# Deltas of all three scan steps on TensorE, key products written in order, and `bn_aggr` for the statistics of the tail

## The reference

```python
def step(S, kvq):
    k_t, v_t, q_t = kvq
    k_norm = k_t / (jnp.linalg.norm(k_t, axis=-1, keepdims=True) + 1e-06)
    retrieved = jnp.einsum('bnij,bnj->bni', S, k_norm)
    delta = v_t - retrieved
    S_new = jnp.tanh(S + jnp.einsum('bni,bnj->bnij', delta, k_norm))
    Sq = jnp.einsum('bnij,bnj->bni', S_new, q_t).reshape(B_, n)
    out = Sq * jax.nn.silu(Sq)
    return (S_new, out)
```

```python
def _layernorm(x, axis=-1, eps=1e-05):
    m = jnp.mean(x, axis=axis, keepdims=True)
    v = jnp.var(x, axis=axis, keepdims=True)
    return (x - m) / jnp.sqrt(v + eps)
```

## Time and profile before

| | before |
|---|---|
| median of 3 runs | 1132.73 us (1132.68 to 1133.84) |
| the profiled execution's own time | 1132.0 us |
| its span, first to last instruction | 1130.1 us |
| mean granted TensorE clock | 0.996 |
| busy share of the span: PE, DVE, ACT, POOL | 97%, 84%, 52%, 45% |

### The profile page before, as it was taken

The page is one execution under the profiler, slowest core; times in us unless marked ns, Lnnn a source line. Parts: engine busy times, 40 slices in busy tenths (PEclk is TensorE's granted clock), DMA queues, the critical chain, the costliest instruction groups (busy, mean ns, idle before and its releaser), DMA issues.

```text
span 1130.1 us, 16851 instructions
## 1 busy us (share of the span) xinstructions
PE 1097.6 (97%) x5925; PEld 855.1 (76%) x5925; DVE 944.7 (84%) x1415; ACT 592.3 (52%) x988; POOL 512.2 (45%) x426
## 2 busy tenths in 40 slices
PE   9999999999999999999999999999999999999786
PEld 4566666678787777878778877878787788778575
DVE  4788888973034998999899889989998998899898
ACT  2345555555435355645655574556456555754544
POOL 1466677676333244324433432443244334364653
PEclk9999999999999999999999999999999999999899
DMA  7346555623531440423132323404231323231001
GB/s 262 109 158 246 205 202 201 247 100 112 168 112 49 139 130 19 130 80 127 56 113 83 123 74 111 148 19 124 81 128 51 116 78 108 75 112 57 1 1 40
DMA packets 45131, 127.03 MB, mean 112 GB/s; under 512 B 4368, under 2 KB 21520, under 8 KB 43152
## 3 DMA queue, kind: packets, MB, share of 16 engines
q1 hardware_dynamic: 43920, 114.20, 30.3%
q10 hardware_dynamic: 1152, 12.07, 2.9%
HBM read 117.86 MB, written 19.92 MB: 122 GB/s over the span
## 4 chain that ended last, share of the span: by engine, by line
PE 73%; DVE 16%; POOL 4%; issue 3%; ACT 2%; DMA 0%; SPq 0%; POOLq 0%; DVEq 0%; ACTq 0%
PE lower L1243 43%; PE bank L1243 17%; PE lower L440 5%; PE lower L572 2%; POOL state L748 2%; POOL rgn L757 2%; PE bank L1232 1%; DVE tmp L2290 1%; DVE tmp L2276 1%; PE bank L487 1%; DVE Sq L2278 1%; DVE tmp L2301 1%; DVE y L847 1%; DVE delta L2297 1%; DVE S L2303 1%
## 5 line engine op out<-in xcount | busy, mean ns | idle before, releaser
L2059 POOL TENSOR_TENSOR a_lo<-whole,a_hi 128x512 fp32r<-128x512 f32 x128 | 181.6, 1435 | 260.3 <-ACT a_hi L1644 172.4
L1243 PE MATMUL lower<-b_hi,ring 128*128 128x512 f32 x512 | 193.8, 396 | 1.4 <-ACT a_hi L1644 1.4
L1243 PE MATMUL lower<-b_lo,ring 128*128 128x512 f32 x512 | 190.9, 391 | 1.7 <-POOL b_lo L2059 1.7
L1243 PE MATMUL lower<-a_hi,ring 128*128 128x512 f32 x496 | 187.5, 394 | 0.0
L1243 PE MATMUL lower<-a_lo,ring 128*128 128x512 f32 x496 | 185.4, 390 | 0.0
L2059 POOL TENSOR_TENSOR b_lo<-whole,b_hi 128x512 fp32r<-128x512 f32 x64 | 93.5, 1469 | 144.4 <-ACT b_hi L1644 125.8
L1627 ACT ACTIVATE S<-S 128x1024 f32<-128x1024 f32 x56 | 58.6, 1059 | 172.8 <-DVE S L2303 168.9
L1643 ACT ACTIVATE whole<-lower,hs 128x512 f32<-128x512 f32 x126 | 86.2, 685 | 81.0 <-PE lower L1243 79.2
L1243 PEld LDWEIGHTS lower<-b_hi,ring 128*128 128x128 f32 x512 | 96.2, 188 | 21.9 <-issue 1.8
L1243 PEld LDWEIGHTS lower<-b_lo,ring 128*128 128x128 f32 x512 | 96.1, 188 | 21.9 <-POOL b_lo L2059 2.3
L440 PE MATMUL lower<-wa,xT 128*128 128x512 f32 x240 | 109.3, 599 | 2.1 <-DVE turned L817 1.4
(11 more groups left out here) (293 smaller groups left out, 2418.8 us busy)
## 6 DMA issues: line engine op xcount, KB each, us to landing
ring<-ffn_copy_dram SPq DMA_DIRECT2D x128, 512.0 KB, 3.5
look<-ffn_dram ACTq DMA_DIRECT2D x6, 1879.0 KB, 6.9
ffn_copy_dram<-ffn_dram SPq DMA_DIRECT2D x4, 2112.0 KB, 9.7
rope<-rope_dram SPq DMA_DIRECT2D x8, 512.0 KB, 8.0
xtok<-x_dram SPq DMA_DIRECT2D x8, 512.0 KB, 4.1
x1in<-x_dram SPq DMA_DIRECT2D x8, 512.0 KB, 4.8
x1res<-x_dram SPq DMA_DIRECT2D x8, 512.0 KB, 3.1
xT<-xT_dram SPq DMA_DIRECT2D x7, 512.0 KB, 8.3
```

Source lines behind the costliest of these rows:

```text
L1243: ins = nc.tensor.matmul(out, a, b, start=(first and n == 0), stop=(last and n == len(pairs) - 1))
L2059: nc.gpsimd.tensor_tensor(lo[:, m, :], t["whole"][:, m % 4, :], hi[:, m, :].bitcast(F32), ALU.subtract).then_inc(lo_done, 1)
```

## The change

It does five things. `times` is now laid out in the order of the state, so that VectorE writes the product with neighbouring columns next to each other, and TensorE reads each plane with a step of 8 columns. `BY_TENSOR` takes in step 0: TensorE makes its two deltas between `turn_left(0)` and `left_keys(0)`, and VectorE's sums and additions of step 0 are gone. GpSimd's reads of steps 0 and 1 wait for the product of the second half. Statistics of the tail go to a tile of their own and are joined by one `bn_aggr` per row, with one small operation for the sign of the mean and one for epsilon; for the last group the mean keeps its sign, and the normalisation subtracts it. The chunks of the main loop keep their statistics.

```diff
-        def row_moments(steps, mv, rows, ve_ready):
+        def row_moments(steps, mv, rows, ve_ready, st, negated=True):
 
             steps.wait()
-            st, sp, m = stats[:, rows], spread[:, rows], mv[:, rows]
-            nc.vector.tensor_tensor(m[:, :, 0], st[:, :, 1], st[:, :, 4], ALU.add)
-            nc.vector.tensor_tensor(sp, st[:, :, 1], st[:, :, 4], ALU.subtract)
-            steps.done(nc.vector.tensor_tensor(m[:, :, 1], st[:, :, 2], st[:, :, 5], ALU.add))
+            for n, b in enumerate(range(rows.start, rows.stop)):
+                ins = nc.vector.bn_aggr(out=mv[:, b, :], in_=st[:, n, :])
+            steps.done(ins)
             steps.wait()
...
-            steps.wait()
-            nc.vector.scalar_tensor_tensor(out=m[:, :, 1], in0=sp, scalar=0.25, in1=m[:, :, 1],
-                                           op0=ALU.mult, op1=ALU.add).then_inc(ve_ready, 1)
+            if negated:
+                nc.vector.tensor_scalar(mv[:, rows, 0], mv[:, rows, 0], -1.0, None, ALU.mult)
+            nc.vector.tensor_scalar(mv[:, rows, 1], mv[:, rows, 1], EPS, None, ALU.add).then_inc(ve_ready, 1)
...
-            tn["times"] = sb(ctx, "times", [P, 2, BS, HALF * BS])
+            tn["times"] = sb(ctx, "times", [P, 2, HALF, BS, BS])
...
-            BY_TENSOR = (1, 2)
+            BY_TENSOR = (0, 1, 2)
...
-                        product(tensor_delta(hf), [(ident[:], x) for x in (v, *(t["times"][:, hf, j, :] for j in range(BS)))]
+                        product(tensor_delta(hf).rearrange("p (n i) -> p n i", i=BS),
+                                [(ident[:], x) for x in (v.rearrange("p (n i) -> p n i", i=BS),
+                                                         *(t["times"][:, hf, :, :, j] for j in range(BS)))]
                                 ).then_inc(fin_delta, 1)
...
                     turn_left(0)
+                    delta(0, 0)
+                    delta(0, 1)
                     left_keys(0)
...
-                            pool.wait_ge(fin_times_k, step_of(s, hf))
+                            pool.wait_ge(fin_times_k, step_of(s, 1 if s in (0, 1) else hf))
...
                     def earlier_moments():
-                        moments(ln3, x3, t["mv3"], ve3)
-                        ln3.end()
+                        st = end_stats[:, 2 * BATCH:3 * BATCH]
+                        ln3.wait()
+                        row_stats(ln3, x3, range(BATCH), st)
+                        row_moments(ln3, t["mv3"], slice(0, BATCH), ve3, st)
...
-                        if s in BY_TENSOR:
-                            w = t["times"][:, hf].rearrange("p j (n i) -> p n i j", i=BS)
+                        w = t["times"][:, hf]
...
-                        row_moments(fin, t["mv3"], rows, ve3)
+                        row_moments(fin, t["mv3"], rows, ve3, st, g < FINAL)
...
                     times_key(0, 0)
                     times_key(0, 1)
-                    sum_times(0, 0)
-                    sum_times(0, 1)
-                    state_delta(0, 0)
-                    state_delta(0, 1)
                     outer(0, 0)
```

More of the change, by code:

```diff
@@ L141, in build, with row_stats @@
         pow_ready = sem(top, "pow_ready")
-        def row_stats(steps, r, rows):
-            for b in rows:
-                ins = nc.vector.bn_stats(out=stats[:, b, :], in_=r[:, b, :])
+        def row_stats(steps, r, rows, st=None):
+            for n, b in enumerate(rows):
+                ins = nc.vector.bn_stats(out=stats[:, b, :] if st is None else st[:, n, :], in_=r[:, b, :])
             steps.done(ins)
@@ L2430, in last_parts @@
                         r = slice(hf * HALF, hf * HALF + HALF)
-                        return k, v, q, last_state(t, hf), deltas[:, r], blocks[:, r]
+                        return k, v, q, last_state(t, hf), blocks[:, r]
                     def earlier_times():
@@ L2542, in times_key @@
                         nc.vector.tensor_tensor(w, st, along_j(k), ALU.mult).then_inc(fin_times_k, 1)
[L2544 to L2555, removed]
-                    def outer(s, hf):
[L2559 to L2564, removed]
+                    def outer(s, hf):
+                        k, _, _, _, w = last_parts(s + 1, hf)
+                        dl = tensor_delta(hf).rearrange("p (n i) -> p n i", i=BS)
+                        dve.wait_ge(fin_delta, delta_of(s, hf))
                         done(nc.vector.tensor_tensor(w, along_i(dl), along_j(k), ALU.mult), "outer", s, hf)
                     def next_state(s, hf):
-                        _, _, _, st, _, w = last_parts(s + 1, hf)
+                        _, _, _, st, w = last_parts(s + 1, hf)
                         after("outer", s, hf)
@@ L2613, in x3_moments @@
                         after("x3", g)
-                        row_stats(fin, x3, range(rows.start, rows.stop))
-                        row_moments(fin, t["mv3"], rows, ve3)
+                        st = end_stats[:, BATCH + rows.start:BATCH + rows.stop]
+                        row_stats(fin, x3, range(rows.start, rows.stop), st)
+                        row_moments(fin, t["mv3"], rows, ve3, st, g < FINAL)
                     def normed_by_hand(g, r, mv, rstd, rooted, count):
@@ L2643, in end_moments @@
                         dve.wait_ge(left_y4, g + 1)
-                        row_stats(fin, left_result(t, g), range(rows.start, rows.stop))
-                        row_moments(fin, left_moments(t, g)[0], rows, ve4)
+                        at = (3 + LEFT[g][0] - d) * BATCH
+                        st = end_stats[:, at + rows.start:at + rows.stop]
+                        row_stats(fin, left_result(t, g), range(rows.start, rows.stop), st)
+                        row_moments(fin, left_moments(t, g)[0], rows, ve4, st, g < FINAL)
                     tail.begin(d)
```

23 lines of the change are left out of this document (10 added, 13 removed).

## The result

The changed kernel takes 1139.34 us (median of 4 runs, 1139.04 to 1139.60), the kernel before 1132.70 (4 runs, 1132.32 to 1133.84): ratio 1.0054 [1.0042, 1.0067]. The forecast was 1129.2 with a range up to 1134.2. It missed by 10.1 us, and on the other side of the kernel before: slower, where a gain was forecast. The profiled execution has a span of 1137.2 us and a time of 1139.04.

What follows compares the result with a forecast made beforehand. VectorE's queue bounds the tail, 1057 to 1126 us. Gains in statistics and products, less losses in steps 0 and 1 and 0.3 at the end, sum to 3.5: 1132.0 - 3.5 = 1128.5, plus 0.7 for the median, 1129.2; range 1128.4 to 1134.2.

Steps and rivals of the forecast that it cites:

- The read of TensorE: TensorE's deltas reading every eighth fp32 column: cost between nothing and 1.4 us per delta, taken as nothing.
- The upper bound: Most that TensorE's strided read could cost, from VectorE's strided write at 0.68 ns per element: 1.4 us per delta.
- rival 1: TensorE's strided read pays 1.4 us in each of six deltas: 3.8 us slower than before, 1136.5 us; chance 0.20.
- Statistics: Tail statistics joined by `bn_aggr`: one-row group 0.44 us, saving 0.41 for one row, 0.33 for two.
- Rival 2: `bn_aggr` costs like `bn_stats`, so 3.4 us of the gain go: 1132.6 us; chance 0.10.
- The products: VectorE's key products, written in order instead of by columns: 1.23 us instead of 1.93, 0.70 less each.
- Rival 3: VectorE's products do not get faster, so 2.5 us of the gain go: 1131.7 us; chance 0.08.
- Step 0: Two deltas moved to TensorE: VectorE waits and lost overlap of 2.98 us against 2.67 taken away, losing 0.31 us.
- The term for the low clock: First delta of step 0 partly at TensorE's 1.2 GHz level, which ends near 1069.2 us: 0.2 us added.
- Step 1: Later `left_keys(0)` delays the tanh; both 0.70 us product gains are lost to waits, a loss of 0.15 us.
- The changed wait of GpSimd: GpSimd's read waits for the second product in step 1; letting it in between would be 1 us worse.
- GpSimd's key root "in time": GpSimd's `key_root` of step 0 ends at 1076.54 us, before VectorE needs it at 1076.75.

Runs made afterwards that it cites:

- pairs: Changed kernel with `times` as four planes of two neighbouring columns, so TensorE reads every second column: 1129.87 us, ratio 0.9969.
- The read by itself: Kernel before, VectorE's writes unchanged, TensorE reading every eighth column in its four deltas, so sums are wrong: 1136.65 us, ratio 1.0035.
- planes: Changed kernel with key products written as before, so TensorE reads neighbouring columns again: 1132.51 us, ratio 0.9997.
- the old wait: Kernel with pairs in all steps, GpSimd's wait of step 1 put back, so its read may start after the first product: 1131.07 us, ratio 0.9980.
- filling: Kernel with pairs in all steps plus seven unread matmuls on TensorE before step 0's deltas: 1129.08 us, ratio 0.9963.
- the new wait of step 1: Kernel before with `bn_aggr` statistics, pairs beyond step 0, and GpSimd's step 1 read waiting for the second product: 1128.05 us, ratio 0.9958.
- runs of four: Changed kernel with `times` as two planes of four neighbouring columns, so TensorE reads every fourth column: 1139.34 us, ratio 1.0053.

## Why the prediction was wrong, point by point

- **The step that failed** is the one headed "The read of TensorE": "I take nothing: a read by TensorE is nearer to its own rows". Measured: 0.12 us per record at full clock, 1.92 per delta. All six deltas take 3.9 us where the walk had 2.0. With pairs, where this cost is gone and all else of the change stays, the time is 1129.87 us against the 1129.2 forecast. From there to the changed kernel are 9.5 us by the medians; the two profiled executions, 7.8 us apart, show 7.5 of them as VectorE's waits for deltas (12.3 against 4.8 us in the lists of waits). The read by itself, in the kernel before, costs 3.8 us with its four deltas.
- **The upper bound failed as well**, which is why rival 1 came true and still missed its number: 1.4 us per delta gave 1136.5, the real 1.92 gave 1139.3, and the range ended at 1134.2, below even rival 1's own number. (The same walk with the measured price, 6 x 1.92 less 1.1 hidden and 3.5 won, is 6.9 us slower than before, 1139.6.) The bound took VectorE's *excess* (0.70 us on 1024 elements, 0.68 ns each) and added it to TensorE's quick rate. In these traces the two engines don't share an excess, they come close in *rate*: VectorE's scattered write runs at 1.93 us / 1024 = 1.88 ns per column, TensorE's scattered read at 0.232 us / 128 = 1.81 ns. By the rate, the prediction's own rows would have given 128 x 1.88 = 0.24 us per record.
- **The Trainium skill, cited beside that step, was right**, and the argument set against it ("another engine's port and the other direction") was only an argument; no row bore it. The chance of 0.20 was too low for that.
- **Statistics**: right. 2.5 us measured alone, 2.4 expected; `bn_aggr` took 0.18 us, and the prediction had taken 0.16. Rival 2 is out. The count of VectorE's instructions falls by 41, from 1415 to 1374, as said.
- **The products**: right, 1.22 us. Rival 3 is out.
- **Step 0**: the form was right, waits of VectorE before both outer products, ended by TensorE. At full clock, with pairs, they are 1.33 and 0.81 us (2.01 and 0.79 predicted, with `turn_left(0)` at the low clock). The term for the low clock was mis-sized: 0.2 us were added, as the stretch was taken to end where it did before. In the profiled executions with planes and with pairs it covers the whole first delta and costs 1.6 us; in those with the old wait and with filling it isn't there at all. The prediction moved every engine's work with the change, and left the clock where it was. Whether moving step 0 to TensorE pays isn't shown: the two waits, 2.14 us at full clock and 4.77 at the low one, stand against 2.67 us of VectorE's work taken away, and the two kernels with pairs and the new wait of step 1 that differ by it (1129.87 and 1128.05 us) lie on two chips with intervals that overlap.
- **Step 1**: right for the changed kernel, in part by luck. The wait before product (1, 1) is 1.11 us, ended by ScalarE, predicted 1.1. But the prediction had it so with deltas of 2.0 us; with pairs at full clock, the case nearest to its walk, it is 0.58 and 0.57 us. The changed wait of GpSimd was put at 1 us; the medians give 1.2 and 1.4, the ratios 1.2 and 0.6.
- **GpSimd's key root "in time"**: it was said to be, by 0.2 us, and a wait of VectorE for it was named as a sign of being wrong. In both kernels with pairs whose first delta ran at full clock that wait is there, 0.43 and 0.45 us. With the old wait of step 1, on VectorE's timeline:

```profile
1077.00 0.56 DVE L2523 RECIPROCAL bank<-norm 128x64 f32<-128x64 f32 x1 [0.43 <-POOL norm L2134]
```

In the changed kernel it doesn't show, as VectorE comes there later, behind its waits for the first deltas. Most of the 0.5 us by which the wait before product (1, 1) shrank went here.

## What to carry to other kernels

A layout that orders one engine's writes scatters another's reads. Cost both sides by the rate that a scattered access shows anywhere in the trace, and not by its excess over the quick form of another engine. Between the two orders there may be one that suits both: here two fp32 columns side by side were enough for the writer and the reader, worth 9.5 us against full order. And where VectorE and GpSimd take turns at SBUF, move the waits with the work. In these traces a product of two SBUF tiles on VectorE that started 0.3 to 0.6 us into a read of GpSimd was held until that ended (3.88 us instead of 1.95, 2.85 and 3.00 instead of 1.23). An outer product, with one input in PSUM, ran its usual 1.23 us beside such a read, in the changed kernel from 1089.74 us, with the read from 1088.45 to 1090.81.

## What was not expected of the hardware

- TensorE's fp32 reads of 128 columns: 0.112 us a record with 4 bytes from column to column, 0.114 with 8, 0.228 with 16 and 0.232 with 32.
- That price is not paid in TensorE cycles. With every eighth column, the 16 records took 3.92 us at 1.2 GHz (clock 0.50 from 1067 to 1073 us) and 3.89 at 2.4 GHz; with pairs 3.62 and 1.98. A scattered read hides the low clock, and a gain from undoing it shrinks where the clock is low: the first delta gained 0.3 us, those of steps 1 and 2 1.9 each.
- The stretches of low clock moved from one profiled execution to the next, in kernels that are alike up to there: at 1054 to 1060 us in some (the old wait, the filled one), at 1067 to 1073 us in others (the changed kernel, planes, pairs), and in both places with runs of four, there from 1068 us.
